# Ternary steps placed more densely ahead of the scan than inside it, and weight pieces loaded ahead of other rows

## The reference, cut to what matters

```python
# layer 0 "attention": a recurrence over 1024 steps for each of 2 batches
k, q = l2norm(h @ Wk.T), l2norm(h @ Wq.T); v = h @ Wv.T
alpha = exp(8 * sigmoid(h @ Wa_w.T + Wa_b) * log(sigmoid(lam) + 1e-8))
def step(H, inp):
    err = sum((v_t - q_t @ H) ** 2); surprise = sigmoid(err)
    delta = k_t[:, None] * (v_t - k_t @ H)[None]
    H = a * H + (1 - a) * surprise * delta
    return H, q_t @ H
# layer 0 feed-forward weights, 2 matrices, groups of 64
scale = clip(mean(|w|), 1e-8); q = clip(round(w / scale), -1, 1)
w_used = w + (q * scale - w)          # bf16
# modulation: (silu(c) @ wmod) gives six vectors a layer, 512 wide
```

## Time and profile before

| | |
|---|---|
| median of 3 runs | 1203.2 us (1203.17 to 1203.88) |
| the profiled execution's own time | 1203.53 us |
| its span | 1201.5 us |
| half-step -18 begins (VectorE L736 of the first group) | 30.66 us |
| half-step 0 begins (VectorE's first L918) | 74.91 us |
| half-step 39 is done (VectorE L950) | 209.43 us |
| TensorE busy over the whole span | 1079.2 us (90%) |

### The profile page before, as it was taken

The page is one execution under the profiler, slowest core; times in us unless marked ns, Lnnn a source line. Parts: engine busy times, 40 slices in busy tenths (PEclk is TensorE's granted clock), DMA queues, the critical chain, the costliest instruction groups (busy, mean ns, idle before and its releaser), DMA issues. The chain is left out here.

```text
span 1201.5 us, 12997 instructions
## 1 busy us (share of the span) xinstructions
PE 1079.2 (90%) x4360; PEld 523.1 (44%) x4360; DVE 873.8 (73%) x1606; ACT 525.1 (44%) x1100; POOL 169.4 (14%) x143
## 2 busy tenths in 40 slices
PE   6678867689998999898899899999998999999997
PEld 3436633444443444344344344444444444444443
DVE  4887775566666788977779699678897587785654
ACT  3656554245543465436255354154435163531421
POOL 3100000011111322122121131222202000200100
PEclk9857768589999999899999899999999999999999
DMA  8511110413230234213220012013020011020000
GB/s 269 176 53 53 36 35 19 175 53 88 88 88 1 68 107 125 78 54 111 73 85 27 19 35 73 25 44 101 27 70 10 1 53 36 18 71 0 1 36 35
DMA packets 47570, 75.53 MB, mean 63 GB/s; under 512 B 8368, under 2 KB 16048, under 8 KB 47376
## 3 DMA queue, kind: packets, MB, share of 16 engines
q1 hardware_dynamic: 47216, 74.62, 19.7%
q0 software_dynamic: 288, 0.09, 0.2%
HBM read 66.16 MB, written 8.54 MB: 62 GB/s over the span
## 5 line engine op out<-in xcount | busy, mean ns | idle before, releaser
L1491 PE MATMUL g_g<-h,wt 128*128 128x512 f16 x1728 | 400.6, 380 | 5.7 <-DVE hid L1794 3.1
L1491 PEld LDWEIGHTS g_g<-h,wt 128*128 128x128 bf16 (+1 forms) x1728 | 167.9, 98 | 223.2 <-issue 33.8
L1505 PE MATMUL g_d<-wt,parts 128*128 128x512 bf16 (+1 forms) x864 | 206.2, 381 | 5.2 <-DVE tmp L1624 2.7
L2114 ACT ACTIVATE parts<-hid 128x512 f16<-128x512 f32 x108 | 68.0, 629 | 303.0 <-DVE hid L1794 303.0
L1414 PE MATMUL g_o<-shared 128*128 128x512 f32 x384 | 183.7, 622 | 14.4 <-DVE tmp L1585 6.4
L1787 DVE SCALAR_TENSOR_TENSOR hid<-th,g_g 128x512 f32<-128x512 f32 x108 | 73.5, 681 | 126.8 <-ACT th L2107 126.7
L1505 PEld LDWEIGHTS g_d<-wt,parts 128*128 128x128 f16 x864 | 83.9, 99 | 113.6 <-issue 16.5
L2224 POOL TENSOR_TENSOR acc<-acc,sqh 128x512 f32<-128x512 f32 x52 | 76.6, 1474 | 299.8 <-ACT sqh L2120 299.8
L1414 PEld LDWEIGHTS g_o<-shared 128*128 128x128 f32 x384 | 75.1, 199 | 99.0 <-issue 72.8
L1799 DVE TENSOR_TENSOR parts<-hid,parts 128x512 f16<-128x512 f32 x108 | 89.7, 831 | 26.0 <-ACT parts L2114 25.9
L2207 POOL TENSOR_TENSOR g_rstd<-g_var,g_power 128x4 f32<-128x4 f32 x20 | 24.2, 1211 | 339.8 <-DVE g_var L1531 339.8
(11 more groups left out here) (319 smaller groups left out, 1522.3 us busy)
## 6 DMA issues: line engine op xcount, KB each, us to landing
shared<-in_w SPq DMA_DIRECT2D x48, 256.0 KB, 2.7
x<-in_codes SPq DMA_DIRECT2D x32, 264.0 KB, 3.1
w_raw<-in_wt SPq DMA_DIRECT2D x16, 512.0 KB, 3.5
x<-in_wmod SPq DMA_DIRECT2D x7, 1024.0 KB, 5.2
wmod<-in_wmod SPq DMA_DIRECT2D x5, 1024.0 KB, 11.6
codes_f<-x SPq DMA_DIRECT2D x32, 132.0 KB, 1.7
gates<-in_x SPq DMA_DIRECT2D x4, 1024.0 KB, 8.6
x<-in_x SPq DMA_DIRECT2D x4, 1024.0 KB, 7.2
```

What stands on the lines that cost most here:

```text
L1491: mm = nc.tensor.matmul(pg[i][:], wide[:, k, o:o + P], h16[f % 2][:, s, k], start=(s == 0 and k == 0), stop=(s == 1 and k == KD - 1))
L1505: mm = nc.tensor.matmul(pd[j][:], parts16[:, t % 3, s, j * P:(j + 1) * P], wd[:, m, :], start=(m == 0 and s == 0), stop=(done and s == 1))
L2114: nc.scalar.activation(parts16[:, t % 3, 0], hid[:, t % 2], ACT.Copy).then_inc(hi_ready, 1)
```

## The change: where the ternary work and the transfers stand

`share` no longer spreads the operations evenly over the 58 half-steps from -18 to 39: a half-step in the front gets 1.5 times as many as one in the scan. The casts and the means follow the same function. And SP's list is put in another order: the weight pieces 2 to 4 are asked for ahead of the rows of the last group, and the modulation weights 2, 3 and 4 each come behind a further piece.

```diff
     def share(h, ops):
 
-        h, n = h - TERNARY_FROM, HALVES - TERNARY_FROM
-        return range(max(0, ops * h // n), max(0, min(ops, ops * (h + 1) // n)))
+        def share_to(h):
+            return max(0, min(ops, ops * (2 * h + min(h, 0) - 3 * TERNARY_FROM) // (2 * HALVES - 3 * TERNARY_FROM)))
+        return range(share_to(h), share_to(h + 1))
 
...
         load_raw(0)
         load_raw(1)
-        load_wmod(2)
         sp.dma_start(keep["wo0"][:], dram["wo0"]).then_inc(wo0_in, 16)
         load_x(2)
-        load_raw(2)
+        for q in range(2, 5):
+            load_raw(q)
         load_x(3)
-        load_wmod(3)
-        load_wmod(4)
-        for q in range(3, PAIRS):
+        for n in range(2, EARLY_SECTIONS):
+            load_raw(n + 3)
+            load_wmod(n)
+        for q in range(8, PAIRS):
             load_raw(q)
```

## The result

| | before | after |
|---|---|---|
| median (9 runs each, side by side) | 1203.88 us (1202.23 to 1206.77) | 1207.51 us (1205.68 to 1209.34) |
| ratio, 95% interval | | 1.0031 (1.0021 to 1.0041) |
| profiled execution, its own time / span | 1203.53 / 1201.5 us | 1207.51 / 1205.4 us |
| half-step -18 to half-step 0 (front) | 44.25 us | 52.57 us |
| half-step 0 to the subtraction of half-step 39 | 132.53 us | 124.52 us |

The change makes the kernel 0.31% slower, 3.7 us, where a change of -0.3 us had been forecast.

The account below looks back on a forecast made before the run. VectorE was taken to bound the front, VectorE and TensorE in turns the scan. Front +4.3 us and scan -4.6 us summed to -0.3: 1202.9 us against the median of 1203.2, 8 in 10 within 1198.5 to 1208.

Parts of the forecast that it names:

- the second item of the front, the waits for the masks: In the front, VectorE's waits for the masks' products were to fall from 2.7 to 1.2 us.
- Half-step -11: In the front, TensorE's chain of some 4 us against 3.5 us of VectorE's work was to leave a 0.5 us wait.
- The waits for means: At piece 0 in the front, two steps now behind each other: VectorE waits 0.6 us for the second mean.
- 11 steps at 0.69 us: In the front, 45 steps in place of 34 were to cost VectorE 7.6 us more.
- The stall near 50 us: In the front, VectorE's 2.37 us wait for squares behind a late cast of piece 3 was to go.
- the 81 that was named as the mark: Half-step 0 was to start at about 79.2 us; before 77.5 or after 81 the front's forecast is wrong.
- The scan: Half-steps 0 to 39 were to become 4.6 us shorter: 4.1 from steps, 1.0 less 0.5 from means.
- the marks of 3 and 7: The scan's forecast is wrong if it shrinks by less than 3 or more than 7 us.
- Half-steps 0, 6, 9, 18, 30 and 36: In the scan, each loses a step without a wait following and pays 0.69 us, 4.1 us in all.
- Half-steps 32 to 34: In the scan, means added in 32 and 34 cost 0.5 us; the step lost in 33 pays nothing.
- ScalarE in step with VectorE: Rival, chance 0.18: in the front ScalarE's casts wait for VectorE's steps, costing some 4 us more, 1206.9 us in all.
- The clock falls otherwise: Rival, chance 0.20, half to each side: TensorE's slow-clock stretches meet other work, giving 1200 or 1206 us.

Follow-up runs that it names:

- second profiles of each: The kernels before and after the change, each profiled again with nothing altered; ratios to before 1.0003 and 1.0031.
- third profile of the kernel after: The changed kernel profiled once more with nothing altered; ratio to before 1.0039.

## Why the prediction was wrong, point by point

**What failed is the second item of the front, the waits for the masks**: "A longer VectorE share in each half-step covers most of it", 2.7 to 1.2 us. They went to 3.9. Half-step -11, sized 0.5 us, came to 0.72; the other four, sized 0.7 together, came to 3.2. A longer share of VectorE does not cover the chain if the chain itself waits for that share. TensorE's mean waits for a ternary step, and TensorE's list is in order, so transposes and products whose inputs are ready stand behind it. More steps in a half-step put the step that releases the mean later by as much as the mask. I had looked for a tighter chain in one half-step, -11, only; the waiting mean stood ahead of three other masks. With the inputs ahead of the means, and nothing else altered, these waits fell to 0.6 us and 0.4.

The Trainium skill (TensorE: Matmul & The Clock Gate, "The mechanism") says that matmuls start and end strictly in the order of the program. The trace agrees: the product at 68.72 started only behind a mean that had waited 2.53 us.

**The waits for means** were sized 0.6 us and measured 1.3 to 1.9. The new wait that was forecast came to 0.65. A second one, which the sum had not looked at, took 0.7 to 1.25 us in the three profiles (1.10 at 46.97 in the first): its mean stood behind 16 projection matmuls of 6.28 us, most of them at 1.2 GHz.

**What held.** 11 steps at 0.69 us: 7.64 us of VectorE's time measured against 7.6. The stall near 50 us: gone with the new order alone, 2.6 us of the front. The sum of the front by measured terms is 7.6 + 1.2 (masks) + 1.3 to 1.9 (means) - 2.4 (stall), 7.7 to 8.3 us; measured on average 8.2, forecast 4.3. The sum of the front was thus 3.9 us too small: 2.7 for the masks and 0.7 to 1.3 for the means. Half-step 0 started at 82.61, past the 81 that was named as the mark for a failure in the front.

**The scan** gave back 6.0 us on average (5.8 in the second profiles of each) where 4.6 was forecast, within the marks of 3 and 7; the first pair alone says 8.0. Half-steps 0, 6, 9, 18, 30 and 36 paid at least 0.7 us each as forecast. 3 paid too, which was to pay nothing, and 26 and 27 together paid 0.9 (8.8 us in place of 9.66 in the second and third profile). In 15 the step was won and lost again in 16. Half-steps 32 to 34, priced at 0.5 us for two more means, took 0.2, 1.3 and 1.5 us more in the three profiles, though a step had left 33. The mean gone from half-step 2 paid 0.43 us, that from 4 nothing (the mask's wait there rose by 0.25). So steps in the scan are worth some 0.5 us apiece (6.0 us for 11, the means included), those in the front 0.98 (10.8 us for 11, against the even spread with the new order).

**The rivals.** ScalarE in step with VectorE gave 1206.9 us, near the result, and for another reason: its waits exist, and removing them left the masks' waits untouched. "The clock falls otherwise" is real, and as far as the runs can tell it is scatter: it moves single profiles by up to 4 us. It is not what makes the kernel slower, since the ratio repeats in three series (1.0031, 1.0031, 1.0039).

**What stays open.** The averages of front and scan give +2.2 us, the timed runs +3.7 to +4.7 (ratios 1.0031 and 1.0039). The first profile's extra 4.2 us behind the head makes up 1.4 of the difference in the average of three; whether the kernel after falls into that more often than the one before, two and three profiles can't tell. And why the projections of half-steps 10 and 11 meet the lower clock in some executions and not in others was not separated from what stands on TensorE there.

## What to carry to other kernels

Filling an engine's idle time with work that another engine's in-order list waits for does not hide that idle time; it moves with the work. Before work is made denser, look in the list of each engine that consumes it for what stands behind the wait, and put first what is ready. The right order is local: the same swap gave 0.1 to 0.2% in the front (1.0031 to 1.0039 against 1.0023, and 0.9987 against 0.997) and took 0.8% with the even spread in the scan, where at the longest wait a 3.5 us projection had come ahead of the mean.

## What the runs showed of the hardware

One program on one core spread over 6 us (1200.5 to 1206.7 for the kernel before, on one chip). Two of its profiles show where: behind the head they agree to 0.01 us (987.70 and 987.71), while the head ended at 213.75 and 216.46 us. Of these 2.7 us, 1.3 lie ahead of half-step -18, 0.1 in the front and 1.3 in the scan. The granted clock was at 1.2 GHz from 48.6 to 106.6 us in the shorter one, and from 51.3 to 95.7 and again from 99.1 to 112.8 in the longer one. The sum of these stretches is nearly the same, 58 us; what differs is which work they meet. The projections of half-steps 10 and 11 fell into the later end, 10.96 us in place of 8.93.

The stretch ahead of half-step -18 shows it most simply, over all 17 profiles of this case, in which the work there hardly differs. Where the granted clock was 1.00 all the way from 14 to 30 us (seven profiles), half-step -18 began at 30.04 to 30.66 us. Where it fell to 0.50 once for a few us between 15 and 21 us (nine profiles), it began at 31.63 to 32.19. In the third profile of the kernel after it stayed at 0.50 longer, from 15.2 to 22.0, and half-step -18 began at 33.43. All four kernels that were profiled more than once stand on both sides, so this belongs to the execution and not to the change.

The piece of weights behind 3 MB showed how fixed a queue's order is. From the issue of piece 3 to its first cast it took 12.4 us in both kernels with the old order (37.99 to 50.36 us before, 40.46 to 52.89 with the new density). So when the casts were due sooner, the whole difference turned into waiting, 5.49 to 9.96 us.
